# A Strassen level, as pairs of 64-column stationaries, in six of the eight blocks of an aggregation

## Chip, core and metric

One core of a Trainium2 chip runs the whole program. Its engines run side by side and meet at semaphores only: TensorE (PE; its weight loads are PEld), VectorE (DVE), ScalarE (ACT), GpSimd (POOL), and SyncE (SP), whose queue issues most of the DMAs. The metric is the device time of one execution in microseconds, as the median of several. All data is fp32.

## The reference, cut to what matters

The program is two layers, each a graph aggregation and a feed-forward part, over 4096 nodes with 128 features. The change touches the last two parts:

```python
def _L1_gnn_ref(input, A, W):
    hidden = input * W
    return A @ hidden                       # (4096 x 4096) @ (4096 x 128)

def _L1_ffn_ref(x, route_id, Wi, bi, Wr, br, Ws, bs, Wo, bo):
    h = relu(flat @ Wi.T + bi)              # 128 -> 256
    for l in range(2):                      # routed layers, 256 -> 256
        shared = h @ Ws[l].T + bs[l]
        routed = h @ Wr[l, e].T + br[l, e]  # e: the expert of the sequence
        h = relu(shared + routed + h)
    return h @ Wo.T + bo                    # 256 -> 128

x = x + _L1_gnn_ref(_layernorm(x), adj, L1_gnn_W)
x = x + _L1_ffn_ref(_layernorm(x)[None], ...)[0]
```

## The kernel before

**Tiling.** The last stage takes the 4096 output nodes in eight blocks of 512. One block's aggregate is a PSUM tile PA of 128 features by 512 nodes. `products3` adds it up from 32 matmuls: the stationary is a tile of S (128 nodes by 128 features of the normalised x), the moving operand is 128 by 512 of the transposed adjacency, from the buffer `ring[1]`. The two PA tiles alternate. The adjacency of a block is 8 MB and comes in four quarters of 2 MB. `ring[1]` holds one block, so the quarter of the next block is loaded into a place as soon as its eight matmuls are done (`refill3`; semaphore `s_quart3`, `s_agg3` for the last quarter).

**The tail of the block before.** Between the matmuls of block k PE does the rest of the work on the rows of block k-1, at places that the table TAIL3 fixes by hand (the number is how many of the 32 matmuls stand in front): at 2 `turn_sum` (four transposes of the scaled aggregate), at 9 `turn_hn3` (four transposes of the normalised rows), at 11 `h0` (the 128 to 256 product), at 14 `layer(k, 0)`, at 16 and 17 `turn_routed`, at 22 `layer(k, 1)`, at 24 and 25 `turn_routed`, at 31 `out_proj`. `layer` is `routed` twice; it already works with 64-column stationaries, two at a time, one into PSUM partitions 0 to 63 and one into 64 to 127 of the same bank, since a sequence has 64 rows.

**The other engines.** Each engine takes its instructions in order. From `turn_sum` to `turn_hn3` runs a chain: DVE adds x to the turned aggregate (L1534) and takes statistics (L948, L951), POOL makes 1/sqrt(var) in two instructions (`inv_sqrt`, L823 and L826), DVE normalises (L1541), and `turn_hn3` waits for that. ACT copies and scales PA (L779), copies hT3 and applies the ReLUs; DVE copies the routed rows out of PSUM (`raw_rows`, L1490).

**SP's queue.** `load_group(k, g)` loads the four expert matrices (256 KB each) of a group; each load is preceded by reading the expert's number into a register. At the stage's start the order is all four groups of block 1, then the four quarters of adjacency block 1.

Of the kernel before, what the change touches and what calls it, by code (L numbers as in the profile page):

```python
# [83 lines left out]
def build(nc, A, out):  # L84
    ctx = ExitStack()
    with ctx:
# [281 lines left out]
        s_agg3 = sem("s_agg3")  # L368
        s_oT = sem("s_oT")
# [71 lines left out]
        def _(sp):  # L441
# [155 lines left out]
            def refill3(b, q):  # L597
                if q < 3:
                    sp.wait_ge(s_quart3, (b - 1) * 3 + q + 1)
                else:  # L600
                    sp.wait_ge(s_agg3, b)
# [9 lines left out]
            for b in range(2, NB + 1):  # L611
                if b < NB:
                    refill3(b, 0)
                load_group(b, 0)
                if b < NB:
                    refill3(b, 1)
                load_group(b, 1)
                load_group(b, 2)
                if b < NB:
                    refill3(b, 2)  # L620
                load_group(b, 3)
                if b < NB:
                    refill3(b, 3)
# [9 lines left out]
        def _(act):  # L633
# [112 lines left out]
            def last_inputs():  # L746

                for h in range(2):
                    nc.scalar.activation(oT[:, h * HW:(h + 1) * HW], PA[1][:, h * HW:(h + 1) * HW], ACT.Copy, scale=w_g[:, 0:1]).then_inc(s_oT, 1)
# [15 lines left out]
            def step3(k, slot, rnd, prev, nxt):  # L765
# [13 lines left out]
                nc.scalar.activation(oT, PA[1 - slot][:, :], ACT.Copy, scale=w_g[:, 0:1]).then_inc(s_oT, 1)  # L779
# [163 lines left out]
        def _(dve):  # L943
# [587 lines left out]
            def inner_step3(k):  # L1531
# [4 lines left out]
                stats(lambda t: x3[:, t * D:(t + 1) * D], BT).then_inc(s_mv4, 1)  # L1536
                dve.wait_ge(s_rstd4, k)
# [5 lines left out]
                for g in range(NG):  # L1543
                    raw_rows(k, g)

            def step3(k):
                if k < NB:
                    inner_step3(k)
                else:
                    last_hn3()  # L1550
# [5 lines left out]
                if k < NB:  # L1556
                    dve.wait_ge(s_fin, k)
                    alone(dve)
# [491 lines left out]
```

## Time and profile before

| | us |
|---|---|
| median of 3 runs | 1009.59 (1009.29 to 1010.35) |
| the profiled execution, its own time | 1014.73 |
| its span in the trace | 1013.0 |
| mean granted TensorE clock over the span | 0.995 |
| PE busy | 988.2 (98%) |
| DVE busy | 345.9 (34%) |
| ACT busy | 310.1 (31%) |
| POOL busy | 178.6 (18%) |

The last stage's matmuls are line L1860: 235.0 us busy in 512 records (a fp32 matmul is two records). They begin at 667 us of the span. To read a timeline row: start, duration of the merged instructions, engine, line, operation, what it writes and reads, rows and columns of the stationary (128*64 is a 64-column one), the moving size, and the number of records. Since matmuls are pipelined, the duration of a merged row is longer than the way to the start of the next one; start to start tells the cost.

### The profile page before, as it was taken

What the parts mean: (1) busy time and instruction counts of PE and PEld (TensorE: products, weight loads), DVE (VectorE), ACT (ScalarE), POOL (GpSimd) and SP (SyncE); (2) the same over time, 40 slices, a digit from 0 to 9 for tenths busy, and PEclk for the clock granted to TensorE, in tenths of its full rate; (3) what the DMA queues carried; (4) which work ended last, traced back from release to release, by engine and by line L of the source; (5) the groups of instructions that cost most, each with busy time, mean ns of one, the idle gap of its engine ahead of it and who ended that gap; (6) DMA issues with size and microseconds to landing.
All of it is one profiled execution on the core that took longest, in us unless ns stands there. A gap on an engine that the chain in (4) does not pass through costs nothing.

```text
span 1013.0 us, 12547 instructions
## 1 busy us (share of the span) xinstructions
PE 988.2 (98%) x3610; PEld 532.2 (53%) x3618; DVE 345.9 (34%) x1322; ACT 310.1 (31%) x601; POOL 178.6 (18%) x216
## 2 busy tenths in 40 slices
PE   8999999999999999999998999979999999999997
PEld 5555555555555444444443688624555454555554
DVE  6323223323323344334434586571121111211114
ACT  4644645645541000000001254232313223132231
POOL 4110010010010122121222165541010110100101
PEclk9999999999999999999999999999999999999999
DMA  9995675366104798888876278279879797797650
GB/s 365 423 413 195 260 318 240 133 291 271 62 0 167 304 338 306 307 308 303 327 278 262 81 241 271 79 211 392 301 286 355 277 367 276 271 372 269 259 167 21
DMA packets 64466, 262.54 MB, mean 259 GB/s; under 512 B 8836, under 2 KB 24904, under 8 KB 52102
## 3 DMA queue, kind: packets, MB, share of 16 engines
q1 hardware_dynamic: 61254, 257.16, 67.1%
q0 software_dynamic: 2864, 4.39, 1.3%
q8 instruction: 28, 0.46, 0.2%
q14 instruction: 48, 0.39, 0.1%
q10 hardware_dynamic: 272, 0.13, 0.0%
HBM read 243.85 MB, written 20.01 MB: 260 GB/s over the span
## 4 chain that ended last, share of the span: by engine, by line
PE 91%; DVE 3%; ACT 2%; issue 2%; DVEq 1%; DMA 1%; POOL 1%; another core or an unknown queue 1%; ACTq 0%; POOLq 0%; SPq 0%
PE PA L1611 22%; PE PA L1631 22%; PE PA L1860 21%; PE O L1806 3%; PE O L1923 3%; PE O L1680 3%; PE T L1943 2%; PE SR L1923 1%; PE O L1652 1%; PE SM L1923 1%; PE PA L1589 1%; PE O L1642 1%; PE O L1901 1%; ACT U L727 1%; PE T L1932 1%
## 5 line engine op out<-in xcount | busy, mean ns | idle before, releaser
L1860 PE MATMUL PA<-ring,S 128*128 128x512 f32 x512 | 235.0, 599 | 4.6 <-issue 3.5
L1631 PE MATMUL PA<-ring,S 128*128 128x512 f32 x512 | 229.8, 595 | 0.9 <-DVE S L968 0.5
L1611 PE MATMUL PA<-ring,U 128*128 128x512 f32 x512 | 226.7, 595 | 0.1
L1611 PEld LDWEIGHTS PA<-ring,U 128*128 128x128 f32 x512 | 94.8, 190 | 106.6 <-issue 106.5
L1631 PEld LDWEIGHTS PA<-ring,S 128*128 128x128 f32 x512 | 95.4, 190 | 101.8 <-issue 98.7
L1860 PEld LDWEIGHTS PA<-ring,S 128*128 128x128 f32 x512 | 92.5, 191 | 104.3 <-issue 100.1
L647 ACT ACTIVATE work<-ring 128x2048 int8<-128x2048 f32 x64 | 122.3, 1910 | 9.2 <-issue 4.9
L904 POOL DMA_INDIRECT y_d<-R,work x40 | 45.3, 1132 | 50.0 <-DVE R L1386 40.5
L795 ACT ACTIVATE work<-T,work 128x64 f32<-128x64 f32 x112 | 29.1, 311 | 64.6 <-PE T L1932 52.1
L892 POOL DMA_INDIRECT disp_d<-work x32 | 31.9, 998 | 96.2 <-DVE work L1308 88.9
L937 POOL DMA_DIRECT2D out_x<-work x7 | 5.9, 837 | 232.7 <-DVE work L1559 232.7
L795 ACT ACTIVATE U<-T,work 128x64 f32<-128x64 f32 x112 | 29.1, 311 | 53.6 <-PE T L1932 39.4
L1132 DVE TENSOR_TENSOR U<-O,b_us 128x256 f32<-128x256 f32 x16 | 6.8, 425 | 90.5 <-PE O L1680 90.5
L660 ACT ACTIVATE work<-work,small 128x256 f32<-128x256 f32 x32 | 16.6, 589 | 68.4 <-POOL small L856 68.4
L697 ACT COPY work<-T 128x512 f32<-128x512 f32 x8 | 4.7, 586 | 106.0 <-PE T L1716 106.0
L1490 DVE COPY U<-O 128x512 f32<-128x512 f32 x16 | 11.1, 692 | 74.2 <-PE O L1923 74.2
L1806 PE MATMUL O<-work,U 128*128 128x128 f32 x280 | 33.1, 278 | 0.5
L851 POOL TENSOR_SCALAR small<-mv 128x4 f32<-128x4 f32 x8 | 1.9, 236 | 179.3 <-DVE small L1119 179.3
L1806 PEld LDWEIGHTS O<-work,U 128*128 128x128 f32 x280 | 31.8, 192 | 2.2 <-issue 1.2
L886 POOL TENSOR_TENSOR small<-small,neg_half 128x4 f32<-128x4 f32 x16 | 16.4, 1024 | 87.4 <-DVE small L1200 77.5
L1923 PE MATMUL O<-ring,work 128*64 128x256 f32 x256 | 29.4, 382 | 0.4 <-ACT work L763 0.4
L695 ACT COPY work<-PA 128x512 f32<-128x512 f32 x8 | 4.7, 586 | 80.0 <-PE PA L1611 51.4
(262 smaller groups left out, 1053.6 us busy)
## 6 DMA issues: line engine op xcount, KB each, us to landing
ring<-in_adj_cols SPq DMA_DIRECT2D x52, 2048.0 KB, 8.8
ring<-in_adjT_cols SPq DMA_DIRECT2D x32, 2048.0 KB, 9.0
ring<-w_d SPq DMA_DIRECT2D x128, 256.0 KB, 3.7
ring<-in_adj_cols SPq DMA_DIRECT2D x8, 1024.0 KB, 12.6
ring<-in_Wr SPq DMA_DIRECT2D x4, 2048.0 KB, 9.4
w_d<-ring SPq DMA_DIRECT2D x8, 1024.0 KB
work<-in_w SPq DMA_DIRECT2D x16, 256.0 KB
disp_d<-U SPq DMA_DIRECT2D x4, 650.0 KB, 19.5
```

The source lines that it names most:

```text
L647: last = nc.scalar.activation(junk, src, ACT.Gelu, scale=GELU_SCALE, accum_out=csum[slot][:, col:col + 1])
L660: last = nc.scalar.activation(zt, zt, ACT.Identity, bias=nm[:, t:t + 1], scale=rstd[:, t:t + 1])
L795: last = nc.scalar.activation(dst[:, m * BW + s * SEG:m * BW + (s + 1) * SEG], src, ACT.Relu, bias=b_r[:, ds(e + (l * KH + m) * E2, 1)])
L892: nc.gpsimd.indirect_dma_start(disp_d, bass.IndirectOffsetOnAxis(ap=idx[:, t:t + 1], axis=0), rows[:, t * ROW:(t + 1) * ROW], None, bounds ...
L904: nc.gpsimd.indirect_dma_start(y_d, bass.IndirectOffsetOnAxis(ap=e_idx[par][:, q:q + 1], axis=0), e_y[par][:, q * D:(q + 1) * D], None, bo ...
L1611: mm = nc.tensor.matmul(out_T[:, :], X[:, t * D:(t + 1) * D], ring[slot][t // HT][:, (t % HT) * BW:(t % HT + 1) * BW], start=n == 0, stop= ...
L1631: mm = nc.tensor.matmul(PA[k % 2][:, :], S[:, t * D:(t + 1) * D], ring[slot][t // HT][:, (t % HT) * BW:(t % HT + 1) * BW], start=t == 0, s ...
L1680: mm = nc.tensor.matmul(o, h1T[:, f * BW + t * P:f * BW + (t + 1) * P], W_us[:, f, :], start=f == 0, stop=f == KH - 1)
L1806: mm = nc.tensor.matmul(bank[:, c * D:(c + 1) * D], e_hm[:, f * CAP + q * P:f * CAP + (q + 1) * P], e_w2[par][:, f * D:(f + 1) * D], start ...
L1860: mm = nc.tensor.matmul(PA[slot][:, :], S[:, t * D:(t + 1) * D], ring[1][t // HT][:, (t % HT) * BW:(t % HT + 1) * BW], start=t == 0, stop= ...
L1923: mm = nc.tensor.matmul(LB[g][c * SEG:(c + 1) * SEG, pair * DH:(pair + 1) * DH], src[:, kk * BW + s * SEG:kk * BW + (s + 1) * SEG], wst[n0 ...
L1943: mm = nc.tensor.matmul(T[t // 2 if k == NB else 0][:, t * D:(t + 1) * D], h_a[:, kk * BW + t * P:kk * BW + (t + 1) * P], w_o[:, kk * D:(k ...
```

## The change

**Strassen level.** For blocks 1 to 6 (`SPLIT`; blocks 0 and 7 stay as they are) the tiles are taken two at a time, and each pair of tiles (256 nodes deep) is a 2x2 product of halves: the features in halves of 64, the block's 512 nodes in halves of 256. Winograd's form has seven half products where there were eight; each is a 64-column stationary with 256 moving columns. They are issued two at a time, into PSUM partitions 0 to 63 and 64 to 127 (`pair`). Four halves of S are formed once (`row_forms`: T1, T2, T3, T4n, four DVE instructions of 1024 elements). The adjacency side is formed for each quarter of each block by four DVE instructions of 1024 elements: `sum_forms`, `cross_forms`, `second_forms`, `third_forms`. Per quarter PE then has `first_pairs` (4 pairs), `cross_pairs` (2), `right_pairs` (4) and `left_pairs` (4).

**Collecting.** ACT copies one quarter result (Eh), DVE adds two (`add_cross`, `add_outer`, 256 columns each), and `select`, four 64-column matmuls with 0/1 matrices, adds them into PA[1]. It stands after `first_pairs` of the next block, and `out_proj` moves with it from the end of block k to after `cross_pairs(k+1, 0)`.

**64-column stationaries elsewhere.** `h0` and `out_proj` are split into pairs of 64 columns too. The transposes stay at 128.

**DVE.** Its program for a block is written out anew (`split_step`), the forms between the old pieces. `sum_forms(k, 2)` stands between the statistics and `normed`.

**SP.** `refill3(1, 0)` moves ahead of the sixteen loads of block 1's experts; `refill3(1, 1)` to `(1, 3)` stay behind them.

```diff
+        def parts(qq):
+            v = ring[1][qq // 2][:, qq % 2 * QUART:(qq % 2 + 1) * QUART].rearrange("p (q j i c) -> p q j i c", q=QP, j=2, i=2, c=SW)
+            return v[:, :, 0, 0, :], v[:, :, 1, 0, :], v[:, :, 0, 1, :], v[:, :, 1, 1, :]
+        SPLIT = range(1, NB - 1)
...
+            refill3(1, 0)
             for g in range(NG):
                 load_group(1, g)
-            for q in range(4):
+            for q in range(1, 4):
                 refill3(1, q)
...
+                    if n == SB and k in SPLIT:
+                        act.wait_ge(s_cross, k)
+                        nc.scalar.copy(Eh, PA[0][:, 0:SW]).then_inc(s_e, 1)
...
+                nc.vector.tensor_tensor(T1, B12, B11, ALU.subtract)
+                nc.vector.tensor_tensor(T3, B22, B12, ALU.subtract)
+                dve.drain()
+                nc.vector.tensor_tensor(T2, B22, T1, ALU.subtract)
+                dve.drain()
+                nc.vector.tensor_tensor(T4n, B21, T2, ALU.subtract).then_inc(s_tform, 1)
...
+                nc.vector.tensor_tensor(S1[c % 2], q21, q22, ALU.add).then_inc(s_form, 1)
...
+                nc.vector.tensor_tensor(q21, q11, q21, ALU.subtract).then_inc(s_form, 1)
...
+                nc.vector.tensor_tensor(S2[c % 2], S1[c % 2], q11, ALU.subtract).then_inc(s_form, 1)
...
+                nc.vector.tensor_tensor(S4[c % 2], q12, S2[c % 2], ALU.subtract).then_inc(s_form, 1)
...
+            def split_step(k):
+                if k > 1:
+                    add_outer(k - 1)
+                sum_forms(k, 1)
+                cross_forms(k, 1)
+                second_forms(k, 1)
+                third_forms(k, 1)
+                if k > 1:
+                    out_rows3(k - 1)
+                aggregate_rows(k)
+                sum_forms(k, 2)
+                normed(k)
+                cross_forms(k, 2)
...
+            def pair(bank, cols, low, low_in, high, high_in, start=False):
+                nc.tensor.matmul(bank[0:HC, cols], low, low_in, start=start, stop=False, skip_group_check=True)
+                return nc.tensor.matmul(bank[HC:P, cols], high, high_in, start=start, stop=False, skip_group_check=True)
...
+            def split_block(k):
+                pe.wait_ge(s_tform, 1)
+                if k > 1:
+                    pe.wait_ge(s_f, k - 1)
+                first_pairs(k, 0)
+                if k > 1:
+                    select(k - 1)
+                cross_pairs(k, 0)
+                if k > 1:
+                    out_proj(k - 1)
+                right_pairs(k, 0)
+                turn_sum(k)
+                left_pairs(k, 0)
+                right_pairs(k, 1)
+                first_pairs(k, 1)
+                turn_hn3(k)
+                cross_pairs(k, 1)
+                left_pairs(k, 1, 0, 1)
+                h0(k)
+                left_pairs(k, 1, 1)
...
-            TAIL3 = [(2, turn_sum), (9, turn_hn3), (11, h0), (14, lambda k: layer(k, 0)), (16, lambda k: turn_routed(k, 0)),
+            TAIL3 = [(2, lambda k: select(k - 1)), (4, lambda k: out_proj(k - 1)), (4, turn_sum), (10, turn_hn3), (12, h0),
```

PE, before, around the end of a block (what is added up moves from PA1 to PA0) (L1860 the aggregation, L1889 `turn_sum`, L1895 `turn_hn3`, L1901 `h0`, L1943 `out_proj`):

```order
L1860 MATMUL PA1<-ring11,S 128x512 x6
L1943 MATMUL T0<-work,U 128x128 x8
L1860 MATMUL PA1<-ring11,S 128x512
L1860 MATMUL PA0<-ring10,S 128x512 x2
L1889 MATMUL T0<-ident,work 128x128 x4
L1860 MATMUL PA0<-ring10,S 128x512 x7
L1895 MATMUL T1<-ident,work 128x128 x4
```

PE, after, at the head of a split block (L2015 and L2016 are the two halves of a `pair`, L2063 and L2066 `select`, L2150 `out_proj`):

```order
L2015 MATMUL PA0<-ring10,S 64x256
L2016 MATMUL PA0<-ring00 64x256
L2063 MATMUL PA1<-W 64x256 x2
L2066 MATMUL PA1<-W 64x256 x2
L2015 MATMUL PA0<-ring10,ring00 64x256
L2016 MATMUL PA0<-ring10,ring00 64x256
L2015 MATMUL PA0<-ring10,ring00 64x256
L2016 MATMUL PA0<-ring10,ring00 64x256
L2150 MATMUL SR<-work,U 64x128 x16
```

`out_proj` went from the end of its block to the head of the next, behind the new `select`, and every product around the transposes is now a 64-column one.

DVE, before, from the turned aggregate to the output rows of one block:

```order
L1534 TENSOR_TENSOR work<-T,R 128x512 [waits s_oTt]
L948 BN_STATS st<-work 128x6 x4
L951 BN_AGGR mv<-st 128x2 x4
L1541 TENSOR_SCALAR work<-work,mv,small 128x128 [waits s_rstd4]
L1541 TENSOR_SCALAR work<-work,mv,small 128x128 x3
L1490 COPY U<-SR 128x512 [waits s_wu]
```

DVE, after, in block 1 (L1602 `sum_forms`, L1606 `cross_forms`, L1612 `second_forms`, L1618 `third_forms`, L1636 the add, L993 and L996 the statistics, L1645 `normed`):

```order
L1602 TENSOR_TENSOR ring<-ring 128x1024 [waits s_ring11]
L1606 TENSOR_TENSOR ring<-ring 128x4x256
L1612 TENSOR_TENSOR ring<-ring 128x1024
L1618 TENSOR_TENSOR U<-ring 128x1024
L1636 TENSOR_TENSOR work<-T,R 128x512 [waits s_oTt]
L993 BN_STATS st<-work 128x6 x4
L996 BN_AGGR mv<-st 128x2 x4
L1602 TENSOR_TENSOR ring<-ring 128x1024 [waits s_ring12,s_quart3]
L1645 TENSOR_SCALAR work<-work,mv,small 128x128 [waits s_rstd4]
```

The add on the turned aggregate now stands behind the four forms of quarter 1, and one form stands inside the chain.

SP, after, at the stage's start (L440 an adjacency quarter, L635 and L636 an expert matrix; fifteen more of these follow before the next L440):

```order
L625 DMA R<-y_d 128x8x128
L440 DMA ring<-in_adjT_cols 128x4096 [waits s_quart3,s_wts3,s_wkept]
L635 TENSOR_LOAD work
L635 ISA x2
L636 ISA
L636 DMA ring<-w_d 128x512
```

Before, nothing that waits for `s_quart3` stood ahead of the expert loads.

## Rows read from the trace of the kernel before

**Rows 1.** The page, parts 1 and 5: busy us (share) and records; busy, mean ns.

```profile
PE 988.2 (98%) x3610; PEld 532.2 (53%) x3618; DVE 345.9 (34%) x1322; ACT 310.1 (31%) x601; POOL 178.6 (18%) x216
...
L1923 PE MATMUL O<-ring,work 128*64 128x256 f32 x256 | 29.4, 382 | 0.4 <-ACT work L763 0.4
```

**Rows 2.** Timeline of PE, one steady block: start us, us, instruction [idle before].

```profile
782.31 0.60 PE L1889 MATMUL T<-ident,work 128*128 128x128 f32 x4
782.74 6.17 PE L1860 MATMUL PA<-ring,S 128*128 128x512 f32 x14
788.75 0.60 PE L1895 MATMUL T<-ident,work 128*128 128x128 f32 x4
...
814.00 5.32 PE L1860 MATMUL PA<-ring,S 128*128 128x512 f32 x12
819.36 2.05 PE L1943 MATMUL T<-work,U 128*128 128x128 f32 x16
821.25 2.74 PE L1860 MATMUL PA<-ring,S 128*128 128x512 f32 x6
823.83 0.60 PE L1889 MATMUL T<-ident,work 128*128 128x128 f32 x4
```

**Rows 3.** Timelines where PE goes between 128- and 64-column stationaries.

```profile
794.77 0.59 PE L1860 MATMUL PA<-ring,S 128*128 128x512 f32 x1
...
795.29 1.30 PE L1923 MATMUL SR<-ring,U 128*64 128x256 f32 x10
...
797.93 1.03 PE L1923 MATMUL SM<-ring,U 128*64 128x256 f32 x8
...
798.90 1.12 PE L1860 MATMUL PA<-ring,S 128*128 128x512 f32 x2
...
999.18 0.82 PE L1923 MATMUL SM<-ring,U 128*64 128x256 f32 x6
...
999.92 0.66 PE L1932 MATMUL T<-ident,U 128*128 128x128 f32 x4
```

**Rows 4.** Timeline of DVE and POOL from `turn_sum` to `turn_hn3`.

```profile
783.06 0.69 DVE L1534 TENSOR_TENSOR work<-T,R 128x512 f32<-128x512 f32 x1 [2.32 <-PE T L1889]
...
784.78 0.38 DVE L951 BATCH_NORM_AGGREGATE mv<-st 128x2 f32<-128x6 f32 x4
...
785.38 0.23 POOL L823 TENSOR_SCALAR small<-mv 128x4 f32<-128x4 f32 x1 [3.19 <-DVE mv L951]
...
785.79 1.04 POOL L826 TENSOR_TENSOR small<-small,neg_half 128x4 f32<-128x4 f32 x1 [0.18 <-POOL small L823]
...
786.98 1.12 DVE L1541 TENSOR_SCALAR work<-work,mv,small 128x128 f32<-128x128 f32 x4 [1.82 <-POOL small L826]
```

**Rows 5.** Timelines of DVE and POOL where both read SBUF at once.

```profile
676.38 0.96 DVE L1452 TENSOR_TENSOR R<-R,S 128x768 f32<-128x768 f32 x1
...
679.66 1.23 DVE L1452 TENSOR_TENSOR R<-R,S 128x1024 f32<-128x1024 f32 x1
```

```profile
676.47 1.74 POOL L910 TENSOR_TENSOR work<-work,neg_half 128x4 f32<-128x4 f32 x1 [0.64 <-DVE work L1466]
```

**Rows 6.** Timelines of PE, ACT and SP's queue at the stage's start; L399 issue to landing.

```profile
675.15 24.30 PE L1860 MATMUL PA<-ring,S 128*128 128x512 f32 x56 [0.22 <-ACT S L742]
699.28 0.60 PE L1889 MATMUL T<-ident,work 128*128 128x128 f32 x4
```

```profile
685.96 3.18 ACT L742 ACTIVATE S<-R,work 128x128 f32<-128x128 f32 x8 [0.97 <-POOL work L917]
```

```profile
667.29 18.90 SPq L595 DMA_DIRECT2D ring<-w_d  x16
686.33 19.13 SPq L399 DMA_DIRECT2D ring<-in_adjT_cols  x5
```

```profile
DMA to landing us min/median/max: 7.7/9.7/12.8
```

**Rows 7.** Busy time by window: length, PE, PEld, DVE, ACT, POOL, granted clock, DMA.

```profile
658.00:661.40 3.40, 0.00 (x0) 0.00 (x0) 0.65 (x4) 0.00 (x0) 1.95 (x2) 1.00 0.02 1
661.40:663.40 2.00, 1.92 (x4) 0.68 (x4) 0.15 (x1) 0.00 (x0) 0.00 (x0) 1.00 0.25 71
663.40:667.00 3.60, 0.10 (x2) 0.07 (x1) 2.65 (x13) 0.00 (x0) 1.28 (x2) 0.93 0.95 262
667.00:670.00 3.00, 3.00 (x4) 1.21 (x5) 2.61 (x12) 0.88 (x2) 1.43 (x3) 0.52 1.14 312
```

More of the change, by code:

```diff
@@ L1532, in inner_step3, with add_outer, aggregate_rows @@
+            def add_outer(b):
+                dve.wait_ge(s_quart3, quarters_done(b, 3))
+                alone(dve)
+                nc.vector.tensor_tensor(Eh[HC:P, :], PA[1][HC:P, SW:BW], Eh[HC:P, :], ALU.add).then_inc(s_ef, 1)
+            def aggregate_rows(k):
                 dve.wait_ge(s_oTt, k + 1)
@@ L1542, in inner_step3, with out_rows3 @@
                 last.then_inc(s_hn3, 1)
[L1543 to L1550, printed above, removed]
+            def out_rows3(k):
                 dve.wait_ge(s_x3b, k)
@@ L1566, in step3 @@
-                dve.drain()
-            for k in range(1, NB + 1):
-                step3(k)
+                dve.wait_ge(s_fin, k)
+                alone(dve)
+                nc.vector.tensor_tensor(ob, SR[:, :], x3, ALU.add).then_inc(s_out, 1)
+                dve.drain()
+            def split_step(k):
[11 more added lines that the diff above has]
+                cross_forms(k, 2)
+                second_forms(k, 2)
+                third_forms(k, 2)
+                sum_forms(k, 3)
+                cross_forms(k, 3)
+                raw_rows(k, 0)
+                raw_rows(k, 1)
+                second_forms(k, 3)
+                third_forms(k, 3)
+                if k + 1 in SPLIT:
+                    sum_forms(k + 1, 0)
+                    cross_forms(k + 1, 0)
+                raw_rows(k, 2)
+                raw_rows(k, 3)
+                if k + 1 in SPLIT:
+                    second_forms(k + 1, 0)
+                add_cross(k)
+                if k + 1 in SPLIT:
+                    third_forms(k + 1, 0)
@@ new lines, in _ @@
+            row_forms()
+            sum_forms(1, 0)
+            cross_forms(1, 0)
+            second_forms(1, 0)
+            third_forms(1, 0)
+            for k in SPLIT:
+                split_step(k)
+            add_outer(NB - 2)
+            out_rows3(NB - 2)
+            aggregate_rows(NB - 1)
+            normed(NB - 1)
+            for g in range(NG):
+                raw_rows(NB - 1, g)
+            out_rows3(NB - 1)
+            last_hn3()
+            dve.wait_ge(s_x3b, NB)
+            alone(dve)
@@ L1572, in _ @@
+            dve.wait_ge(s_stored, (NB - 1) * 16)
+            alone(dve)
+            for h in range(2):
+                at = slice(h * BW // 2, (h + 1) * BW // 2)
+                dve.wait_ge(s_fin, NB + h)
+                alone(dve)
+                nc.vector.tensor_tensor(ob[:, at], T[h][:, at], x3[:, at], ALU.add).then_inc(s_out, 1)
+            dve.drain()
         @block.tensor
@@ L1900, in h0 @@
                 for m in range(KH):
-                    last = nc.tensor.matmul(O[m][:, :], w_i[:, m * P:(m + 1) * P], hT3, start=True, stop=True)
+                    for h in range(2):
+                        at = m * P + h * HC
+                        last = nc.tensor.matmul(O[m][h * HC:(h + 1) * HC, :], w_i[:, at:at + HC], hT3, start=True, stop=True)
                 last.then_inc(s_h0p, 1)
```

205 lines of the change are left out of this document (158 added, 47 removed).

## Prediction

> **What bounds the kernel now.** I read the page first: PE is busy 98% of the span, no other engine over half [rows 1]. So a term counts only where it changes PE's own work or makes PE wait. Next, PE's timeline through one block: from one `turn_sum` (782.31) to the next (823.83) is 41.52 us, with no idle but 0.2 us [rows 2]; that period is what the change alters, six times. Then what stands beside it: the chain of DVE and POOL instructions from `turn_sum` to `turn_hn3` [rows 4], and the start of the stage, where the first split block begins [rows 6].
>
> **Products: -3.3 us a block.** Seven 128-column matmuls take 782.74 to 788.75, 0.859 each; 32 are 27.5 us [rows 2]. For a pair of 64-column stationaries the trace has the same shape (128*64, 256 moving) in the routed layer. Its eight-record row lasts 1.03 us; less the 0.38 of one record that is three steps of 0.216, and a pair is two steps, 0.432 us [rows 1, 3]. (The two halves run side by side: one after the other they would take 0.86.) A block has 14 pairs a quarter, 56, that is 24.2 us. The pairs differ from the routed ones only in what they read, so I take the row as it is.
>
> **Select: +0.86.** Two pairs of the same shape, 2 x 0.432.
>
> **Going between 64 and 128 columns: +1.1.** The trace has each step. Into 64: 794.77 to 795.29 is 0.52 where 0.43 is due, +0.09; the ten-record row is (1.30 - 0.38)/4 = 0.23 a step, so its first step cost +0.05: 0.14. Out to a transpose: the six-record row's last step begins at 999.18 + 0.82 - 0.38 = 999.62, the transposes at 999.92, 0.30 where 0.216 is due, +0.09, and the four transposes take 0.66 for the usual 0.60, +0.06: 0.15. Out to a 512-column matmul: +0.09, and 1.12 - 0.59 = 0.53 for 0.43, +0.10: 0.19 [rows 2, 3]. Before, a block has two islands of 64 columns: 2 x 0.33 = 0.7. After, it has six islands of 128, the transposes: 6 x 0.29 = 1.75. The Trainium skill, in "TensorEngine Tiling (Array Packing)", section Key Properties, says that a change of tiling mode drains TensorE. The 0.09 us at each change agree; by the rule alone, without these prices, this term would be unknown in size but not in sign.
>
> **h0 and out_proj: -0.3.** `h0` stays two steps' worth of 512 columns, no change. `out_proj` now takes 819.36 to 821.25, 1.89, after a wait of 0.2 for the last ReLUs (the row before should end at 814.00 + 12 x 0.43 = 819.15) [rows 2]. As 16 steps of a pair with 128 moving columns it costs 16 x 0.109 = 1.75 if the halves run side by side (0.109 is a transpose's start-to-start, 0.43/4), and 3.5 if they don't. I take 1.75, since the routed pairs do; 3.5 stays an upper end, +1.75 in each of seven. It also stands 1.5 us later behind the ReLUs, so the 0.2 goes.
>
> **Sum without waits.** Blocks 2 to 6: -3.3 + 0.86 + 1.1 - 0.3 = -1.7 each, -8.5. Block 1 has no `select` and no `out_proj`, which move to the next block: -3.3 + 1.1 - 2.1, and +0.14 to enter: -4.2. Block 7, still 128 columns, gets `select` and a second `out_proj` (0.86 + 1.75) and about eight single changes more (1.3): +3.9. Together -8.8 us. Half of what the seventh product saves is spent again on changes and on `select`.
>
> **The forms: 0 on DVE, but they sit in a chain.** A form of 1024 elements is 1.23 us [rows 5]; sixteen a block and the small adds are 21 us. Beside DVE's 6 us of old work that fits into 40, and walking the order through, each form is ready several us before its pairs, with 3.5 us or more for every quarter's reload too. What hides them is DVE's 34 us of idle time a block. One place is tight. Before, the chain from `turn_sum` to the end of the normalising is 782.31 to 786.98 + 1.12 = 788.10, 5.8 us, and PE reaches `turn_hn3` at 788.75, 6.4 [rows 2, 4]. After, PE has `turn_sum` (0.43 + 0.06), 12 pairs (5.18) and two changes (0.23): 5.9. The chain alone would just fit (5.97 with 0.15 for the semaphore). But `sum_forms(k, 2)` now runs while POOL wants to do its two instructions. The trace shows what that does: the same four-element power takes 1.04 us alone [rows 4] and 1.74 beside a 768-element add of two SBUF operands that began 0.1 before it [rows 5]. The add had 0.87 us to go; POOL lost 0.70. With a 1.23 us form that began 0.1 earlier POOL loses about 1.23 - 0.13 - 0.17 = 0.9, or 0.7 if its first short instruction slips in ahead. I take 0.85. PE waits 0.85 in blocks 2 to 6: **+4.3**. The Trainium skill, "SBUF — State Buffer", section Who interferes with whom, states it as a lock: a VectorE instruction with two SBUF inputs and a GpSimd one that reads SBUF exclude each other for a whole instruction. The row agrees; by the rule the loss would be 1.1 rather than 0.9 at most. In block 7 no form stands there, but the gap is only six matmuls (5.15 + 0.49) and `out_rows3` is ahead on DVE: +0.5.
>
> **Block 1: +6.1.** Block 0 ends two matmuls before 699.28, at 697.56. ACT's last hidden tile is ready at 685.96 + 3.18 = 689.14 [rows 6]. `row_forms` and the first three forms of quarter 0 are seven DVE instructions, about 1.25 apart: 698.1, so PE starts +0.5 late. Then SP. `refill3(1, 0)` waits for the eighth matmul of block 0: 675.15 starts the seventh, so 677.0. Sixteen expert loads stand behind it, which took 18.9 us with the first few slow and 1.1 each otherwise [rows 6]: 17.7, so that `refill3(1, 1)` is issued at about 695.4 where that of before left the queue with the row of 686.33. With the shortest landing seen, 7.7 [rows 6], quarter 1 is there at 703.1. DVE's four forms of it take 5.0: 708.1. Only behind them stands the add on the turned aggregate, though `turn_sum` is done at 703. The chain from that add to the end of the normalising is 5.0 [rows 4], with POOL's 0.85: 714.1. PE gets to `turn_hn3` at 698.1 + 4.4 + 5.9 = 708.5. It waits 5.6 us; queued behind that wait are the rest of the block, and with it everything.
>
> **The clock: +1.6.** That wait is longer than any in the stage now. After two idle stretches of 3.5 us, at 658 and 663.4, the granted clock was 0.52 from 667 to 670 [rows 7], that is the 1.2 GHz level; after the first of the two alone it was still 1.00. Three us at half speed lose 1.5. With 5.6 us of idleness I expect the same fall: 1.6.
>
> **Sum.** -8.8 + 4.3 + 0.5 + 6.1 + 1.6 = +3.7 us. On the profiled execution, 1014.73, of which 1013.0 are span, that is 1018.4. Its time is 0.5% over the median of the runs, 1009.59, and I carry the difference over: 1013.3, rounded to **1013**. A difference of 0.2% (2 us) is about what a measurement of this kernel can tell from none.
>
> **Rivals.**
> 1. *The chain does not hold PE up (faster).* If POOL's two instructions come through beside the form, as they do when DVE is still at its semaphore waits when POOL starts, the 4.3 us go; if the wait of block 1 then also shrinks by POOL's share and by a quicker landing, it is too short for the clock to fall, another 1.6 to 2.5. 1013.3 - 4.3 - 2.2 = 1006.8. For it: the chain fits within 0.1 us without POOL's loss. Against: the row of the power instruction at 1.74. It decides from a loss below 0.2 us. Chance 0.20.
> 2. *As forecast, but the clock stays up.* 1013.3 - 1.6 = 1011.7, or 1011.2 with a landing a little sooner: within 0.2%. For it: the first of the two idle stretches left it at 1.00. Chance 0.23.
> 3. *128-column pairs don't run side by side (much slower).* `out_proj` costs 3.5: 7 x 1.75 = 12, so 1025. Against: the 256-column ones do. That the pairs of the aggregation didn't, so that the change would not do what it says, would cost 24 us a block; the routed rows exclude it nearly. Chance 0.06 for both.
> 4. *Forecast, 1013, with the waits up to 3 us longer*, should DVE's other waits (`raw_rows`, `add_cross`) bite: chance 0.51 with the forecast itself.
>
> **Numbers.** Faster 0.20 (rival 1), same 0.25 (rival 2 and the forecast's lower edge), slower 0.55 (the rest). The range reaches from rival 1, 1006.8, to the forecast with 3.5 us more, 1016.5, and leaves out rival 3 and half of what lies below rival 1's figure.
>
> **What would show it.** In the profile after: a pair of products 0.43 us from start to start and `out_proj` 1.75; six gaps of 0.1 us around transposes; the power instruction of POOL at about 1.7 to 1.9 us (or its first one long) and PE idle some 0.85 us before `turn_hn3` in blocks 2 to 6; one idle stretch of 5 to 6 us at 708 to 714, behind DVE instructions that waited for the second quarter's DMA; then 3 us at a granted clock near 0.5; periods of 40.7 us in blocks 2 to 6 where they were 41.5. The prediction is wrong if the period comes out near 39.8, if block 1 shows no such gap, or if another wait appears that the rows of before have no sign of.

## The result, and the profile after

| | timed runs, us | profiled execution: own time, span |
|---|---|---|
| before | 1009.88 median (1009.29 to 1010.35, 4 runs) | 1014.73, 1013.0 |
| after | 1017.5 median (1016.69 to 1018.05, 4 runs) | 1017.69, 1015.9 |

The change makes the kernel slower: ratio 1.0074, 95% interval 1.0062 to 1.0087, 7.6 us. I had forecast slower, by 3.7.

Line numbers of the new code: the 128-column products are now L2007, the pairs L2015 and L2016, `turn_sum` L2091, `turn_hn3` L2097, `h0` L2105, `turn_routed` L2137, `out_proj` L2150; `turn_sum_half`, the first thing behind the split blocks, is L2073. The page of after, parts 1 and 5 (as [rows 1]):

```profile
PE 985.6 (97%) x4782; PEld 560.0 (55%) x4782; DVE 475.7 (47%) x1438; ACT 313.1 (31%) x607; POOL 188.5 (19%) x216
...
L2016 PE MATMUL PA<-ring 128*64 128x256 f32 x480 | 118.7, 385 | 0.0
L2015 PE MATMUL PA<-ring,S 128*64 128x256 f32 x384 | 92.0, 382 | 0.8 <-DVE ring L1612 0.8
```

PE is busy 2.6 us less than before, in a span 2.9 us longer. So the work did shrink, and the loss is waiting. (Busy time hides part of the loss: matmuls at half clock count as busy.) The waits of PE, whole span, first row of the view (total, times, longest):

```profile
PE T L2097 <- DVE work L1645: 9.3, 7, 5.2
```

Seven waits at `turn_hn3`, none of which stood there before: 5.15 us in block 1, 0.74 in each of blocks 2 to 6, and 0.40 in block 7.

**A steady block.** PE's timeline of after in block 4 (as [rows 2, 3]; start, us, instruction, idle before it):

```profile
830.09 0.66 PE L2091 MATMUL T<-ident,work 128*128 128x128 f32 x4
...
836.82 0.66 PE L2097 MATMUL T<-ident,work 128*128 128x128 f32 x4 [0.74 <-DVE work L1645]
...
847.60 0.38 PE L2016 MATMUL PA<-ring 128*64 128x256 f32 x1
847.91 0.66 PE L2137 MATMUL T<-ident,U 128*128 128x128 f32 x4
848.49 0.43 PE L2015 MATMUL PA<-ring,S 128*64 128x256 f32 x1
...
848.76 0.38 PE L2015 MATMUL PA<-ring,S 128*64 128x256 f32 x1
...
848.98 0.38 PE L2015 MATMUL PA<-ring,S 128*64 128x256 f32 x1
...
867.16 1.92 PE L2150 MATMUL SR<-work,U 128*64 128x128 f32 x32
868.91 0.38 PE L2015 MATMUL PA<-ring 128*64 128x256 f32 x1
...
870.74 0.33 PE L2091 MATMUL T<-ident,work 128*128 128x128 f32 x1
```

The block takes 870.74 - 830.09 = 40.65 us, where it was 41.52 [rows 2]. A step of the pairs is 848.98 - 848.76 = 0.22, with L2015 and L2016 side by side. An island of transposes takes 848.76 - 847.60 = 1.16 from the step before it to the second behind, where two steps and four transposes would be 0.43 + 0.43 = 0.86: 0.30 for its two changes. `out_proj` takes 868.91 - 867.16 = 1.75. And between the two turns stands the wait: 836.82.

DVE and POOL between those two turns (as [rows 4]):

```profile
832.62 0.38 DVE L996 BATCH_NORM_AGGREGATE mv<-st 128x2 f32<-128x6 f32 x4
...
832.96 1.23 DVE L1602 TENSOR_TENSOR ring<-ring 128x1024 f32<-128x1024 f32 x1
...
833.21 1.07 POOL L868 TENSOR_SCALAR small<-mv 128x4 f32<-128x4 f32 x1 [2.23 <-DVE mv L996]
...
834.46 1.03 POOL L871 TENSOR_TENSOR small<-small,neg_half 128x4 f32<-128x4 f32 x1 [0.18 <-POOL small L868]
...
835.65 1.11 DVE L1645 TENSOR_SCALAR work<-work,mv,small 128x128 f32<-128x128 f32 x4 [1.46 <-POOL small L871]
...
836.68 1.22 DVE L1606 TENSOR_TENSOR ring<-ring 128x1024 f32<-128x1024 f32 x1
...
836.94 2.09 POOL L977 TENSOR_TENSOR work<-work 128x512 f32<-128x512 f32 x1 [1.44 <-DVE work L1645]
...
837.99 2.12 DVE L1612 TENSOR_TENSOR ring<-ring 128x1024 f32<-128x1024 f32 x1
```

POOL's first instruction (four elements) took 0.23 before [rows 4]; here it runs to 834.28, beside the form L1602, which ends at 834.19: 1.07. The power behind it is unchanged at 1.03. The normalising L1645 starts some 0.8 later for it, and `turn_hn3` with it.

**Block 1.** DVE and PE (as [rows 6]):

```profile
701.05 1.23 DVE L1602 TENSOR_TENSOR ring<-ring 128x1024 f32<-128x1024 f32 x1 [5.17 <-DMA ring<-in_adjT_cols]
...
705.96 0.68 DVE L1636 TENSOR_TENSOR work<-T,R 128x512 f32<-128x512 f32 x1
```

```profile
699.18 0.66 PE L2091 MATMUL T<-ident,work 128*128 128x128 f32 x4
...
702.33 0.43 PE L2015 MATMUL PA<-ring 128*64 128x256 f32 x1 [0.62 <-DVE ring L1602]
...
704.78 0.43 PE L2015 MATMUL PA<-ring,S 128*64 128x256 f32 x1 [0.50 <-DVE ring L1612]
...
711.88 0.90 PE L2097 MATMUL T<-ident,work 128*128 128x128 f32 x3 [5.15 <-DVE work L1645]
```

DVE stood for 5.17 us until quarter 1 had landed; PE waited 0.62, 0.50 and 5.15 us for what DVE made of it. SP's queue shows why the quarter came late: it stood behind the sixteen expert loads.

```profile
674.03 0.35 SPq L440 DMA_DIRECT2D ring<-in_adjT_cols  x1
675.42 17.36 SPq L636 DMA_DIRECT2D ring<-w_d  x16
692.91 1.97 SPq L440 DMA_DIRECT2D ring<-in_adjT_cols  x3
```

Behind the idle stretch the clock fell. Windows of after (as [rows 7]: length, busy time of PE, PEld, DVE, ACT, POOL, granted clock, DMA):

```profile
706.50:711.80 5.30, 0.23 (x4) 0.00 (x0) 3.67 (x15) 0.00 (x0) 2.11 (x2) 0.95 1.01 433
711.80:714.90 3.10, 3.02 (x14) 1.94 (x16) 3.01 (x3) 0.58 (x1) 2.08 (x1) 0.50 0.88 375
714.90:718.10 3.20, 3.20 (x12) 0.98 (x12) 1.49 (x2) 0.00 (x0) 0.00 (x0) 0.50 0.03 10
718.10:721.30 3.20, 3.20 (x30) 1.96 (x28) 1.15 (x2) 1.26 (x2) 0.00 (x0) 1.00 0.30 61
```

The granted clock was at 0.50 (the 1.2 GHz level) from 711.8 to 718.1, though PE worked without a break from 711.88 on.

**Where the time went.** From one turn to the next, read from PE's timelines of each kernel (us):

| | turn_sum to turn_hn3, block 1 | block 1 | blocks 2 to 5, each | turn_sum(1) to L2073 (before: L1870) |
|---|---|---|---|---|
| before | 6.45 | 41.51 | 41.51 | 289.57 |
| after | 12.70 | 49.61 | 40.65 | 292.58 |

Block 0 ended 1.72 us ahead of turn_sum(1) before (two 128-column products) and 4.89 after (ten pairs of block 1). So from the end of block 0 to L2073 the stage takes 291.29 before and 297.47 after: +6.2. Block 0 itself (30.59) and all that stands behind L2073 (24.1) take the same in both.

### The profile page after: what moved, and what is told of

Its sections match the earlier page's. It is cut to its first block, busy times and chain, and to the rows that moved or that the text cites. A ratio compares the mean times of both kernels' runs of the same rounds, so it can differ in the third digit from the quotient of the medians.

```text
span 1015.9 us, 15120 instructions
## 1 busy us (share of the span) xinstructions
PE 985.6 (97%) x4782; PEld 560.0 (55%) x4782; DVE 475.7 (47%) x1438; ACT 313.1 (31%) x607; POOL 188.5 (19%) x216
## 4 chain that ended last, share of the span: by engine, by line
PE 82%; DVE 4%; ACT 3%; issue 3%; POOL 2%; DMA 2%; SPq 2%; DVEq 1%; POOLq 0%; ACTq 0%
PE PA L1758 22%; PE PA L1778 22%; PE PA L2015 11%; PE O L1953 3%; ACT U L769 3%; PE O L2128 3%; PE O L1827 3%; PE PA L2007 3%; PE T L2137 2%; PE O L1799 1%; PE PA L1736 1%; PE SR L2128 1%; PE SM L2128 1%; PE O L2105 1%; PE SR L2150 1%
## 5 line engine op out<-in xcount | busy, mean ns | idle before, releaser
L1778 PE MATMUL PA<-ring,S 128*128 128x512 f32 x512 | 229.8, 595 | 1.7 <-DMA ring<-in_adj_cols 1.7
L1778 PEld LDWEIGHTS PA<-ring,S 128*128 128x128 f32 x512 | 95.3, 190 | 103.0 <-issue 100.1
L2016 PE MATMUL PA<-ring 128*64 128x256 f32 x480 | 118.7, 385 | 0.0
L2015 PE MATMUL PA<-ring,S 128*64 128x256 f32 x384 | 92.0, 382 | 0.8 <-DVE ring L1612 0.8
L2015 PE MATMUL PA<-ring 128*64 128x256 f32 x288 | 73.0, 387 | 0.6 <-DVE ring L1602 0.6
L2015 PEld LDWEIGHTS PA<-ring,S 128*64 128x64 f32 x384 | 51.6, 137 | 32.7 <-issue 7.2
L2007 PE MATMUL PA<-ring,S 128*128 128x512 f32 x128 | 59.9, 613 | 4.2 <-issue 3.3
L2016 PEld LDWEIGHTS PA<-ring 128*64 128x64 f32 x480 | 63.2, 137 | 0.0
L2015 PEld LDWEIGHTS PA<-ring 128*64 128x64 f32 x288 | 37.5, 138 | 21.6 <-issue 4.6
L2016 PE MATMUL PA<-U,S 128*64 128x256 f32 x192 | 47.1, 383 | 0.0
L2007 PEld LDWEIGHTS PA<-ring,S 128*128 128x128 f32 x128 | 23.6, 195 | 33.8 <-issue 29.7
L1602 DVE TENSOR_TENSOR ring<-ring 128x1024 f32<-128x1024 f32 x24 | 29.4, 1225 | 25.1 <-PE PA L2016 19.8
```

Source lines behind the costliest of these rows:

```text
L1778: mm = nc.tensor.matmul(PA[k % 2][:, :], S[:, t * D:(t + 1) * D], ring[slot][t // HT][:, (t % HT) * BW:(t % HT + 1) * BW], start=t == 0, s ...
L2007: mm = nc.tensor.matmul(PA[bank][:, :], S[:, t * D:(t + 1) * D], ring[1][t // HT][:, (t % HT) * BW:(t % HT + 1) * BW], start=t == 0, stop= ...
L2015: nc.tensor.matmul(bank[0:HC, cols], low, low_in, start=start, stop=False, skip_group_check=True)
L2016: return nc.tensor.matmul(bank[HC:P, cols], high, high_in, start=start, stop=False, skip_group_check=True)
```

## Experiments

Theory A of all of them: the change pays for three separate things, a quarter that comes late in block 1 (with the clock behind it), a form beside POOL's instructions in every block, and the changes between 64 and 128 columns. The rivals name another place for the loss, or say that a price is only in the records and not in the time. Each ratio is to the kernel before in the same session; the change alone is 1.0074.

### The SP order of block 1: `sp_mixed`

```diff
-            refill3(1, 0)
-            for g in range(NG):
-                load_group(1, g)
-            for q in range(1, 4):
+            for q in range(NG):
                 refill3(1, q)
+                load_group(1, q)
```

> The changed kernel with one edit: at the start of the last stage SP issues the quarters of adjacency block 1 and the four groups of expert loads in turn (quarter 0, group 0, quarter 1, group 1, ...), so that quarter 1 is issued behind 4 expert loads and not behind 16. Theory A (the arrival of quarter 1 holds DVE, DVE holds the add on the turned aggregate, and PE waits at the first turn_hn3): quarter 1 is there before DVE asks for it, the idle stretch of 5.2 us in block 1 shrinks to 0.8 to 2, the two short ones ahead of it (0.6 and 0.5) go, and with them the half clock of 6.7 us behind it; together -8 to -9.5 us, about 1008.5. Rival (the DVE work itself, five forms of 1.2 us between the products and the add, is what PE waits for): the wait stays above 4 us and the time falls by 1 to 2 us at most.

Measured: 1012.08 us, ratio 1.000 (0.9990 to 1.0009). Block 1 takes 40.82 us instead of 49.61, with 6.89 between its turns, and the granted clock stays at full speed there. The waits of PE, first row, beside after's 9.3 in total and 5.2 at most:

```profile
PE T L2095 <- DVE work L1643: 5.0, 7, 0.9
```

8.8 us went in block 1, and 7.5 in the timed runs (1.0074 to 1.000), by moving transfers alone. This edit moves the quarters 2 and 3 and the expert loads too; the next two runs move quarter 1 by itself. The rival, that the forms themselves hold PE, would have left a wait of over 4 us: it is 0.9.

### How late may the quarter be: `q1_after_12`, `q1_after_8`

The edit of `q1_after_12`; `q1_after_8` has `range(2)` in the first loop and the groups 2 and 3 behind the refill.

```diff
-            for g in range(NG):
+            for g in range(3):
                 load_group(1, g)
-            for q in range(1, 4):
+            refill3(1, 1)
+            for g in range(3, NG):
+                load_group(1, g)
+            for q in range(2, 4):
                 refill3(1, q)
```

> The change with quarter 1 of block 1 issued on SP behind 12 expert loads of the block instead of 16 (the last four, group 3, come behind it). An expert load held SP's queue 1.09 us (16 of them from 675.42 to 692.8 us), so the quarter is issued 4.4 us earlier, at about 688.5, and the chain quarter, forms, L1636, statistics, normed, turn_hn3(1) should end 4.4 us earlier. Theory A (the wait is all that chain's, and TensorE's clock falls only after a long idle stretch): from turn_sum(1) to turn_hn3(1) 8.3 us instead of 12.7, idle ahead of turn_hn3(1) 1 to 2 us, no half clock behind it, block 1 at 42.2 us instead of 49.6; 7.4 us less, ratio 1.0000. Theory B (the clock falls after any wait of more than 1 us in this place): 4.4 us less, block 1 at 45.2 us, ratio 1.003. Theory C (landing takes as long as the expert loads ahead of the quarter need to drain, so earlier issue brings little): 2 us less or nothing, block 1 over 46.

> The change with quarter 1 of block 1 issued behind 8 expert loads, 8.7 us earlier than in the change, at about 684.2 us. Theory A: the chain of the quarter ends before TensorE comes, turn_sum(1) to turn_hn3(1) 6.7 us as in blocks 2 to 6, no half clock, block 1 at 40.8 us, 8.8 us less than the change, ratio 0.9987, the same as with the fully mixed order. Theory C: with the experts' transfers in front the quarter lands no earlier than 3 us before it did, block 1 at 44 us or more. Theory D (now groups 2 and 3 of the experts come too late for the layers of block 1): a wait on an expert transfer in block 1's layers, of up to the quarter's issue time, 2.3 us.

`q1_after_12`, PE, SP's queue and windows:

```profile
PE T L2100 <- DVE work L1648: 6.4, 7, 2.3
```

```profile
676.21 12.58 SPq L636 DMA_DIRECT2D ring<-w_d  x12
688.91 0.35 SPq L440 DMA_DIRECT2D ring<-in_adjT_cols  x1
```

```profile
705.00:708.20 3.20, 0.96 (x10) 0.36 (x6) 2.27 (x6) 0.00 (x0) 1.20 (x2) 1.00 1.00 425
708.20:711.60 3.40, 3.36 (x24) 1.91 (x26) 3.24 (x2) 0.59 (x1) 2.09 (x1) 1.00 1.03 439
```

| | quarter 1 behind | turn_sum to turn_hn3 | half clock | block 1 | ratio (95%) |
|---|---|---|---|---|---|
| change | 16 loads | 12.70 | 6.8 us long | 49.6 | 1.0074 (1.0062 to 1.0087) |
| `q1_after_12` | 12 | 8.26 | none | 42.17 | 1.0035 (1.0019 to 1.0051) |
| `q1_after_8` | 8 | 7.42 | none | 41.34 | 1.0000 (0.9991 to 1.0009) |
| `sp_mixed` | 4 | 6.89 | none | 40.82 | 1.0000 (0.9990 to 1.0009) |

Four loads fewer ahead took 4.44 us out of the gap, as theory A had it (8.3 and 42.2 were expected), and the half clock went with an idle stretch of 2.3 us instead of 5.15. In the timed runs less came back: 1.0035, where A gave 1.0000 and B 1.003. The profiled execution (1011.13) was the second fastest of eight, which reach to 1016.68. That the quarter lands later in the others and brings part of the wait and the half clock back would explain it, and isn't shown. So for 12 loads rival B, by which the half clock stays, is out for the trace and not for the timed runs.

With 8 loads ahead the gap is still 0.7 us over the 6.73 of a steady block. DVE's rows show both what is left and a new order on POOL:

```profile
698.11 1.23 DVE L1621 TENSOR_TENSOR U<-ring 128x1024 f32<-128x1024 f32 x1
699.25 0.68 DVE L1639 TENSOR_TENSOR work<-T,R 128x512 f32<-128x512 f32 x1
...
701.72 1.23 DVE L1605 TENSOR_TENSOR ring<-ring 128x1024 f32<-128x1024 f32 x1 [0.37 <-DMA ring<-in_adjT_cols]
...
701.97 1.86 POOL L874 TENSOR_TENSOR small<-small,neg_half 128x4 f32<-128x4 f32 x1 [0.18 <-POOL small L871]
```

The last form of quarter 1 (L1621) still stands in front of the add L1639, which starts 1.52 us behind `turn_sum` (697.73) where it is 0.80 in block 4 (830.89 - 830.09): that is the 0.7. POOL's price is the 0.8 of the steady blocks, only on the other instruction: the form of quarter 2 waited 0.37 for its DMA, so POOL's first instruction (0.24) was through before it and the power took 1.86 beside it.

### SP order in the kernel before: `before_sp`

The other side of the same question. The kernel before, with quarter 0 of its first loop ahead of the expert loads, as the change has it.

> The kernel before with the changed order of SP's queue alone: refill3(1, 0) ahead of the sixteen expert loads, the other three quarters behind. Theory A: the late quarter 1 harms only because DVE's forms stand ahead of the add; here PE reads it itself at its ninth product, 7.3 us into block 1, about when it lands: 0 to +0.7 us, the same as before (1009.9). Rival (the order costs by itself, by later loads of all quarters): +3 us or more with waits of PE for the adjacency in block 1. Also looked at here: at what time of the span the stage's first product starts (667.0 in the profile of before, 663.7 in that of the change), in a program of before's length.

Measured: 1013.16 us, ratio 1.0013 (1.0000 to 1.0026). The order itself costs some 1.3 us (0 to 2.6) where no forms stand between the quarter and its products; in the trace block 1 takes 42.50 us instead of 41.51, 0.7 of it a wait of PE for quarter 1. It is the forms, and the add and the statistics queued behind them, that make the late quarter dear. The stage's first product starts at 663.53 here, as in after (663.70) and not as in before (666.97); so that difference isn't the change's.

### The clock by itself: `warm`

Six matmuls of 128x512 on data that is there, with a result that nothing reads, ahead of `turn_hn3(1)`.

```diff
                 first_pairs(k, 1)
+                if k == 1:
+                    keep_warm(6, S[:, 0:BW], O[0])
                 turn_hn3(k)
```

> The changed kernel with one edit: six 128x512 matmuls with the identity into an unused PSUM bank stand ahead of turn_hn3(1), 5.2 us of work that nothing reads, in the place of the idle stretch. The wait itself stays. What goes is the half clock behind it. Theory C: the granted clock was about 0.5 from 708.5 to 718.6 or so, PE worked at that level for 6.7 us and lost 3.0 us; with PE busy the clock stays at 1.00 and the time falls by 2.5 to 3.2 us, about 1014.7. Rival (my forecast of 1.6 us for the clock was right and the rest of the 3 us is another wait in block 1): the time falls by 1.6 us or less and the way from turn_hn3 to h0 stays longer than the 1.9 us of the other blocks.

Measured: 1020.27 us, ratio 1.008 (1.0058 to 1.0103). The gain of 2.5 to 3.2 us that was expected lies outside this interval, so in the timed runs it is a miss. The trace has the part that was asked for:

```profile
712.57 5.42 PE L1736 MATMUL O<-S,ident 128*128 128x512 f32 x12
...
717.82 0.63 PE L2097 MATMUL T<-ident,work 128*128 128x128 f32 x4
```

```profile
717.80:721.20 3.40, 3.40 (x25) 1.90 (x26) 3.22 (x3) 0.59 (x1) 2.09 (x1) 1.00 0.09 39
```

The clock is 1.00 from `turn_hn3(1)` on, and from there to the next `turn_sum` it is 33.89 us, as in steady blocks (33.92), against 36.91 in after: in the trace the clock's price is 3.0 us. But in this execution the quarter, issued at 696.50, was read by DVE only at 706.96, 10.5 us later, where in after it was 8.1 (692.91 to 701.05), and `turn_sum` to `turn_hn3` grew from 12.70 to 15.03. The added matmuls did not delay that, since they start at 712.57. Whether the quarter also landed late in the timed runs, and why, isn't known; the price of the clock rests on the trace alone.

### The wait behind POOL: `form_after`

```diff
-                sum_forms(k, 2)
                 normed(k)
+                sum_forms(k, 2)
                 cross_forms(k, 2)
```

> The changed kernel with one edit: sum_forms(k, 2) stands behind the normalising on DVE, no longer between the statistics and it. Theory L (POOL's small instruction cannot read SBUF while a form with two SBUF inputs runs on DVE): POOL's L868 falls from 1.07 us back to 0.23, the wait before turn_hn3 in blocks 2 to 6 from 0.81 to 0.1 or less, the period of a block from 40.65 to 39.9, and the time by 6 x 0.8 = 4 to 5 us, about 1013. Rival (the wait is only the longer DVE queue, and the form costs the same wherever it stands near): POOL's instruction stays long beside some other form, or the wait moves to first_pairs(k, 2) or left_pairs; the time stays within 1 us.

Measured: 1015.57 us, ratio 1.0036 (1.0019 to 1.0053). Blocks 2 to 5 take 39.85 us each instead of 40.65. DVE and POOL in block 4:

```profile
833.64 0.38 DVE L996 BATCH_NORM_AGGREGATE mv<-st 128x2 f32<-128x6 f32 x4
...
834.22 0.23 POOL L868 TENSOR_SCALAR small<-mv 128x4 f32<-128x4 f32 x1 [2.23 <-DVE mv L996]
...
834.64 1.04 POOL L871 TENSOR_TENSOR small<-small,neg_half 128x4 f32<-128x4 f32 x1 [0.18 <-POOL small L868]
```

One form, moved by one place, and the first instruction is back at 0.23; the period falls by 0.80, which over five blocks is 4.0, and the ratio by 0.0038 (1.0074 to 1.0036). That is the wait of the prediction's chain, and its cause.

### Mode changes: `grouped`

```diff
                 first_pairs(k, 2, 0, 2)
                 turn_routed(k, 0)
-                first_pairs(k, 2, 2)
                 turn_routed(k, 1)
+                first_pairs(k, 2, 2)
...
                 turn_routed(k, 2)
-                right_pairs(k, 3, 0, 2)
                 turn_routed(k, 3)
-                right_pairs(k, 3, 2)
+                right_pairs(k, 3)
```

> The change with one edit: in each of blocks 1 to 6 turn_routed(k, 1) stands directly behind turn_routed(k, 0), and turn_routed(k, 3) behind turn_routed(k, 2), so that two islands of 128-column transposes fewer stand among the 64-column pairs. Theory A (each island costs its two mode changes, 0.14 us in and 0.15 us out): 0.58 us less in each block, a period of 40.07 us instead of 40.65, 3.5 us less over six blocks, ratio to the kernel before 1.0039. Theory B (the mode changes cost nothing, the first steps behind them only look longer in the records): period 40.65, ratio 1.0074. Theory C (turn_routed(k, 1) now waits for its copy out of PSUM, which ended at 847.99 against a first transpose at 847.90 in block 4): the period falls by less than 0.3 us, and a wait on that copy appears.

Measured: 1019.97 us, ratio 1.0043 (1.0025 to 1.0061). PE's timeline:

```profile
808.33 0.38 PE L2016 MATMUL PA<-ring 128*64 128x256 f32 x1
808.64 1.09 PE L2137 MATMUL T<-ident,U 128*128 128x128 f32 x8
809.66 0.43 PE L2015 MATMUL PA<-ring,S 128*64 128x256 f32 x1
...
809.93 0.38 PE L2015 MATMUL PA<-ring,S 128*64 128x256 f32 x1
```

The period is 40.05, 0.60 less for two islands: 0.30 each, where the prediction has 0.29. The ratio is 0.0029 below that of `change_again` in the same session (0.0035 was expected). Theory B, that the longer first steps are only in the records, is out.

### The change again, and the edits together: `change_again`, `sp_and_form`, `all_three`

> The changed kernel itself once more, as it stands, timed beside the kernel before on the chip of the other runs of this job. Theory A (the wait in block 1 and the half clock behind it are what the change pays, always): ratio 1.0074 again, in the trace 49 to 50 us from block 1's turn_sum to block 2's, with 4 to 6 us idle ahead of turn_hn3(1) and 6.8 us of half clock from there. Theory B (part of the first result was the chip or the one profile): ratio between 1.003 and 1.006, and block 1 within 3 us of the others. In both, blocks 2 to 6 take 40.65 us.

> The change with two edits that were tried one by one: the SP order quarter 0, group 0, quarter 1, group 1 and so on for block 1, and sum_forms(k, 2) behind normed(k) on VectorE. Theory A (two separate losses): both gains add, 8.8 us and 4.0 us, block 1 takes 40.0 us and blocks 2 to 6 take 39.85; ratio to before 1.0074 - 0.0087 - 0.0040 = 0.9947. Theory B (once block 1's wait is gone the forms that stand later on VectorE hold the pairs of quarter 2): block 1 or all blocks 0.5 us or more over that, ratio 0.997 or more.

> The change with all three edits: SP order of block 1, sum_forms(k, 2) behind normed(k), and the turn_routed steps in twos. Theory A (three separate losses): period 39.27 us, no half clock in block 1, ratio 0.9947 - 0.0035 = 0.991, some 9 us faster than the kernel before. Theory B (mode changes cost nothing): as with two edits, 0.9947. Theory C (TensorE, with less between its waits, comes earlier than VectorE or the adjacency's quarters): a wait of 0.3 us or more a block on a form or on a DMA appears, ratio above 0.993.

| | median, us | ratio (95%) | expected | block 1 | blocks 2 to 5 |
|---|---|---|---|---|---|
| before, same session | 1015.86 | | | | |
| `change_again` | 1022.06 | 1.0072 (1.0046 to 1.0097) | 1.0074 | 49.57 | 40.65 |
| `sp_and_form` | 1008.67 | 0.9934 (0.9908 to 0.9959) | 0.9947 | 40.53 | 39.85 |
| `all_three` | 1007.0 | 0.9917 (0.9893 to 0.9941) | 0.991 | 39.92 | 39.23 |

The losses add up, so they are separate. With all three gone the kernel is 0.8% faster than before. Its block 4 is full (a window of that one block, as in [rows 7]):

```profile
821.27:860.50 39.23, 39.23 (x362) 25.75 (x361) 27.15 (x36) 11.22 (x37) 5.31 (x4) 1.00 0.89 333
```

PE is busy for all 39.23 us, with DVE at 27.15: no form and no DMA holds it.

`change_again` also tells what a single profile is worth. The wait of PE on a DMA ahead of the stage, in the profiled execution of before (that of `change_again` has the same, at its L1736):

```profile
PE PA L1589 <- DMA y_d<-R,work: 3.5, 1, 3.5
```

After's first profile has no such wait, and its stage starts 3.3 us earlier: 6.2 - 3.3 = 2.9, the difference of the spans 1013.0 and 1015.9. In `change_again` the stage starts at 666.66, near before's 666.97, and the spans are 1018.8 - 1013.0 = 5.8 apart, near the stage's 6.2.

## Why the prediction was wrong

The sign was right, and the traces show each mechanism that the prediction named; the size was not: +3.7 forecast, +7.6 measured (+6.2 in the stage by the traces). The time, 1017.5, lies 1.0 us above the range. Two terms of the sum were too small: the wait in block 1, 5.6 us, measured 6.8, and the clock, 1.6 us, measured 3.0. Point by point:

| step | forecast | measured | from |
|---|---|---|---|
| a pair of products | 0.432 | 0.43 | two steps of 0.216 |
| one island's changes | 0.29 | 0.30 | `grouped`: 0.60 for two |
| `out_proj` | 1.75 | 1.75 | timeline of after |
| period of blocks 2 to 5 | 40.7 | 40.65 | timeline of after |
| wait at `turn_hn3`, blocks 2 to 6 | 0.85 each | 0.80 each | `form_after` |
| block 1's first pair late | 0.5 | 0.28 | 694.71 - 694.29 - 0.14 |
| wait at `turn_hn3`, block 7 | 0.5 | 0.40 | waits of after |
| wait in block 1 | 5.6 | 6.8 | 12.70 - 5.9 |
| clock behind it | 1.6 | 3.0 | 36.91 - 33.92; `warm` 33.89 |

**Sum without waits, and POOL's wait: right.** Rival 1 falls, since the chain does hold PE. Only the instruction differs: I priced the loss on the power and named the first short one as the other case; in after it was the short one in all six split blocks (median 1.07), which comes 0.25 us into the form. By the lock of the Trainium skill ("SBUF — State Buffer", Who interferes with whom) POOL's instruction would wait for the rest of the form, 834.19 - 833.21 = 0.98, and then take its 0.23: 1.21. The trace has 1.07, so it waits as the rule says, and a little less. The trace has the same in turn behind it: POOL's add L977, which took 1.27 in the kernel before, took 2.09 beside the form L1606 that had begun 0.26 before it, and the form L1612, begun meanwhile, took 2.12 instead of 1.22. That costs nothing here because both have the time.

**Block 1: the step "It waits 5.6 us" failed by 1.2.** The course of it is what the prediction has, from the sixteen loads to the idle PE. What was too small is the moment at which quarter 1 can be read. Counted from the end of block 0 (697.56 in the prediction, 694.29 in after) it was to be there at +5.5, and DVE started on it at +6.8. The larger part is the refill's issue, 0.8 later than worked out (+0.3 until quarter 0 left the queue, and 18.9 instead of 18.4 from there: 1.4 us passed between quarter 0 and the first expert load, where I had 0.7 in all). The other 0.4 is the landing: issue to first use took 8.1 where I had put 7.7, the shortest of [rows 6]. In the five executions with this order of SP's queue it took 8.1, 8.5, 8.6, 9.0 and 10.5 (after, `change_again`, `grouped`, `form_after`, `warm`), so the best case of the view was under them all. Its median, 9.7, would have made the wait 7.6, the forecast 1015.3 and the range wide enough, but by luck: it is over four of the five.

**The clock: the step "I expect the same fall" failed by 1.4.** I took [rows 7], where three us at the low level cost 1.5. Here the low level lasted from 711.25 to 718.08, 6.8 us, and cost 3.0. It was 6.8 us in all four executions in which the clock fell in block 1 (after, `change_again`, `grouped` and `form_after`, with 4.3 to 5.2 us of idleness ahead of `turn_hn3`). That the longer idle stretch is the reason isn't shown, and other places speak against it. At the stage's start PE stands 3.3 to 3.7 us in all executions but one; the low level there lasted 3.4 us in before and after, and 6.8 in `sp_mixed`, `change_again` and `grouped`. At 554 us, where the change touches nothing, it lasted 6.8 us in before and 10.2 in after. Windows of `sp_mixed` (idle for 3.45 until 663.20) and of after:

```profile
664.50:671.00 6.50, 6.06 (x7) 2.38 (x8) 5.63 (x29) 2.97 (x8) 3.98 (x5) 0.50 0.35 97
```

```profile
555.00:564.00 9.00, 8.48 (x18) 3.81 (x19) 3.53 (x25) 1.82 (x5) 2.79 (x4) 0.50 0.01 2
```

So [rows 7] showed one size out of several that a fall has, the smallest, and I took it as the price. This term should have had an upper end of its own. Rival 2, that the clock stays up, came true only once the wait was cut to 2.3 us.

**The two terms together are 2.6 us, and the stage's miss is 6.2 - 3.7 = 2.5.** The small terms cancel: the other waits came out 0.6 us smaller (0.3 in blocks 2 to 6, 0.2 at block 1's first pair, 0.1 in block 7), which leaves some -8.3 for PE's own work where the sum has -8.8.

**What stays open: 1.4 us.** The first timed runs are 7.6 us apart and the stage accounts for 6.2. The interval of the ratio is 6.3 to 8.8 us, and in the second session the medians were 6.2 apart, so this may be nothing. (The ratio of that session, 1.0072, would make it 7.3.) I found no place for it. Ahead of the stage the profiled executions differ by as much where the change touches nothing: the first product of the program starts at 8.26 in before, 9.37 in after and 8.11 in `change_again`, and PE's work around the low clock at 554 us takes 19.06 us in after (552.74 to 571.80) and 17.71 in before (551.64 to 569.35). Whether that falls differently on the two kernels in the timed runs isn't shown.

**Median and profile.** Carrying the 0.5% between before's profile and its median over to the forecast did no harm that shows: the profile had the 3.5 us wait of the DMA above, and the timed runs, it seems, mostly do not.

The range was too narrow at the top. Its "3.5 us more" had to hold landing, clock and other waits at once; a landing at the median (+2.0) with a clock at twice (+1.6) is 3.6 already, and the two are not independent: the same late landing makes the wait and brings the clock down behind it.

## What to carry to other kernels

When a change puts a new reader in front of a transfer, go through the queue that issues the transfer again, order by order: the saving in TensorE's work here (8.8 us by the sum, some 8.3 by the traces) was no larger than what one refill behind sixteen small loads cost (8.8 us with the clock, by `sp_mixed`), and moving the loads gave it back for nothing. Price a wait by the spread of the landings and not by the shortest (here 8.1 to 10.5 us in five executions), with all that the queue issues ahead of it. Price a fall of the clock together with the wait in front of it, and by more than one stretch of the trace: in this program the low level lasted 3.4, 6.8 or 10.2 us. Where a critical chain goes through POOL, keep long two-input SBUF instructions of DVE out from beside it, and put the 128-column steps among 64-column pairs next to each other: one place moved in an order was worth 0.80 us a block, and one island less 0.30.

## What the runs showed of the hardware

- The low level of TensorE's clock lasted 3.4, 6.8 or 10.2 us in these traces, and not the same in the same place: at the stage's start, behind 3.3 to 3.7 us of idleness, 3.4 us in before and 6.8 in `change_again`; at 554 us 3.4 in `sp_mixed`, 6.8 in before and 10.2 in after. In block 1 it was 6.8 us behind idle stretches of 4.3 to 5.2, and in after PE worked without a break through the last 6.2 us of it. Behind 2.3 us of idleness in `q1_after_12` it did not come, but in `all_three` it did at 662.3, behind 2.1 us. Six matmuls in the idle stretch of block 1 kept it away there.
- Of DVE (with two SBUF inputs) and POOL the one that comes second waits, whichever it is: 0.23 became 1.07 on POOL, a power of 1.04 became 1.86, an add of 1.27 became 2.09, and 1.22 became 2.12 on DVE. In `form_after` two forms of DVE without a gap between them (836.86 and 837.99) held the same add for both: 3.22 us.
- Pairs of 64-column stationaries in fp32 run side by side for 128 moving columns too: sixteen steps of `out_proj` in 1.75 us. A change between 64 and 128 columns and back costs 0.30 us (`grouped`: 0.60 for two).
- An expert load of 256 KB, with the reading of the expert's number, holds SP's queue for 1.05 to 1.09 us (17.36 for 16, 12.58 for 12), so sixteen of them put 17 us between one refill and the next.
